# Two edits to a one-core kernel: when the next context is asked for, and how the first query is laid out

## What is computed

```python
h = jnp.concatenate([x, latents], axis=1)                 # 375 context rows, 112 latents
q = (latents @ q_w + q_b).reshape(b, k_len, NH, DH)       # 16 heads of 32
kv = (h @ kv_w + kv_b).reshape(b, p + k_len, NH, DH, 2)
attn = jnp.einsum('bkhd,bnhd->bhkn', q, kmat) / DH        # mask, softmax over n
attn_out = jnp.einsum('bhkn,bnhd->bkhd', attn, v).reshape(b, k_len, H)
attn_out = attn_out @ out_w + out_b + residual            # then RMS norm, MLP, + residual
```

## Time and profile before

| | us |
|---|---|
| median of three runs | 907.5 |
| lowest, highest | 907.29, 908.57 |
| the profiled execution | 907.18 |
| its span in the trace | 905.4 |
| PE busy | 857.8 (95%) |
| DVE, ACT, POOL busy | 567.1 (63%), 429.4 (47%), 228.5 (25%) |
| mean granted TensorE clock | 0.989 of full |

### The profile page before, as it was taken

The page is one execution under the profiler, slowest core; times in us unless marked ns, Lnnn a source line. Parts: engine busy times, 40 slices in busy tenths (PEclk is TensorE's granted clock), DMA queues, the critical chain, the costliest instruction groups (busy, mean ns, idle before and its releaser), DMA issues.

```text
span 905.4 us, 16349 instructions
## 1 busy us (share of the span) xinstructions
PE 857.8 (95%) x6220; PEld 671.0 (74%) x6220; DVE 567.1 (63%) x1318; ACT 429.4 (47%) x965; POOL 228.5 (25%) x242
## 2 busy tenths in 40 slices
PE   6777999999999988999999999999989999999998
PEld 5766777686867765676787777877767677888987
DVE  3499999999999989552233453333434365544654
ACT  3313242424242445344666685757656885333342
POOL 3546556464646458200000000000000000110100
PEclk9988999999999999999999999999999999999999
DMA  7657645554637253104002020202140231000200
GB/s 272 164 117 207 186 138 148 147 150 134 158 114 189 81 153 78 49 19 106 18 9 86 9 63 1 63 1 63 30 185 1 105 133 64 1 0 0 82 0 35
DMA packets 44421, 80.51 MB, mean 89 GB/s; under 512 B 21485, under 2 KB 27629, under 8 KB 42558
## 3 DMA queue, kind: packets, MB, share of 16 engines
q1 hardware_dynamic: 39742, 77.71, 29.8%
q10 hardware_dynamic: 4608, 1.84, 0.8%
HBM read 70.36 MB, written 9.18 MB: 88 GB/s over the span
## 4 chain that ended last, share of the span: by engine, by line
PE 46%; ACT 3%; DMA 1%; issue 1%; DVE 1%; SPq 0%; DVEq 0%
PE bank L1856 9%; PE bank L1843 8%; PE bank L1717 8%; PE bank L1723 7%; PE bank L1809 4%; PE bank L1801 3%; PE bank L1828 3%; PE bank L1765 2%; PE bank L1751 2%; ACT smb L1300 2%; DMA cx<-latc_scratch 1%; ACT pts L1308 1%; PE bank L1475 0%; PE bank L1817 0%; ACT cx_hi L1190 0%
## 5 line engine op out<-in xcount | busy, mean ns | idle before, releaser
L900 DVE CUSTOM_DVE_ANT_0 smb<-bank,mask 112x487 f32<-112x487 f32 x128 | 78.1, 660 | 126.1 <-issue 126.0
L693 DVE TENSOR_TENSOR_SCAN scan<-bank,scan 128x448 f32<-128x448 f32 x128 | 132.0, 1073 | 5.8 <-POOL scan L547 4.9
L1481 PEld LDWEIGHTS bank<-xj,front 128*128 128x128 f32 x1024 | 119.6, 196 | 10.1 <-issue 8.1
L544 POOL TENSOR_TENSOR scan<-scan,ks 128x896 f32<-128x896 f32 x64 | 124.2, 1940 | 2.3 <-DMA scan<-v_scratch 2.2
L1481 PE MATMUL bank<-xj,front 128*128 128x112 f32 x1024 | 121.9, 280 | 1.5 <-POOL xj L535 1.5
L1300 ACT ACTIVATE smb<-smb,nmax 112x487 f32<-112x487 f32 x128 | 88.3, 691 | 64.9 <-DVE nmax L900 64.5
L521 POOL TENSOR_TENSOR small<-small,neghalf 112x1 f32<-112x1 f32 x24 | 13.4, 559 | 362.4 <-DVE small L936 268.1
L700 DVE TENSOR_TENSOR scan<-scan,bank 128x896 f32<-128x896 f32 x64 | 68.8, 1078 | 1.8 <-PE bank L1481 1.0
L535 POOL TENSOR_TENSOR xj<-tmp,xa 128x448 f32<-128x448 f32 x40 | 42.4, 1062 | 86.1 <-DVE tmp L662 86.1
L1121 ACT ACTIVATE bank<-ws 128x448 f32<-128x448 f32 x32 | 17.5, 548 | 91.1 <-DVE scan L693 77.2
L1809 PE MATMUL bank<-ident,smb 112*122 112x112 f32 x512 | 56.6, 262 | 3.9 <-ACT smb L1300 3.5
(11 more groups left out here) (196 smaller groups left out, 1760.8 us busy)
## 6 DMA issues: line engine op xcount, KB each, us to landing
scan<-v_scratch SPq DMA_DIRECT2D x64, 448.0 KB, 5.5
cx<-in_ctxt SPq DMA_DIRECT2D x8, 750.0 KB, 5.2
raw_w<-in_wbig SPq DMA_DIRECT2D x4, 1024.0 KB, 7.8
w<-in_w SPq DMA_DIRECT2D x2, 2048.0 KB, 7.4
w<-in_w SPq DMA_DIRECT2D x1, 3328.0 KB, 11.7
tail<-in_wbig SPq DMA_DIRECT2D x3, 1024.0 KB, 9.2
front<-in_wbig SPq DMA_DIRECT2D x2, 1024.0 KB, 9.9
x_f<-in_x SPq DMA_DIRECT2D x8, 224.0 KB, 6.3
```

The costliest lines, as they stand in the source:

```text
L544: g.tensor_tensor(buf[:, :, :], buf[:, :, :], ks[b % 2][:, k:k + 1, 0:T].broadcast_to([P, VS, T]), ALU.mult).then_inc(s["a_ready"], 1)
L693: n = v.tensor_tensor_scan(flat, decay, flat, 0.0, ALU.mult, ALU.add)
L900: v.tensor_tensor_reduce(sm[r], bank[r][0:T, 0:NKEY], mask_b[b % 2][:, :], -1.0 / DH, 3e38, ALU.add, ALU.min, nmax[:, h:h + 1]).then_inc(s ...
L1481: i = t_.matmul(tiles(dst)[:, m, :], w[:, k, m * P:(m + 1) * P], x[:, k, :], start=k == 0, stop=k == NT - 1)
```

## The change

1. In SP's loop `load_context(b + 2)` moves from the end of the body to its top, ahead of `load_latents(b)`. Its own waits are the same.
2. `first_query` exchanges the operands. The stationary operand is now the latents (128 by 112), the moving one the 512 columns of a row of tiles of `qw`. The result is the query with tokens on partitions, in 12 products. ACT copies it to SBUF (`q_rows`, which lies where `lt` will be later), and PE turns it by four transposes (`first_query_turned`) into the same bank as before. On PE the transposes stand between `hidden_gate` and `hidden_values`. On ACT the copy stands where the bias was added; the bias now stands behind `second_gate`.
3. The pairs of semaphores `st`/`mv` of the layer norms become one each (`row_stats`), waited for at 2b + 1 and 2b + 2 in place of b + 1 of either. No instruction comes or goes by that.

```diff
@@ SP, the loop over the attentions
             for b in range(1, B - 1):
+                if real(b + 2):
+                    load_context(b + 2)
                 load_latents(b)
...
                 if real(b + 2):
-                    load_context(b + 2)
                     load_mask(b + 2)
@@ ACT
+            def first_query_rows():
+                act.wait_ge(s["q_rows"], 1)
+                c_.copy(q_rows[:, :], bank[7][0:T, :]).then_inc(s["q_rows_kept"], 1)
...
                 relu_squares(a_)
+                first_query_rows()
+                second_gate(a_)
                 first_query_columns()
-                second_gate(a_)
@@ PE
-                for m in range(NT):
-                    for k in range(NT):
-                        for w, c in in_parts(parts("qw"), x):
-                            i = t_.matmul(tiles(7)[:, m, :], w[:, k, m * P:(m + 1) * P], c[:, k, 0:T],
-                                          start=k == 0 and w is w_hi["qw"] and c is x[0],
-                                          stop=k == NT - 1 and w is w_lo["qw"])
-                i.then_inc(s["qp_ready"], 1)
+                for k in range(NT):
+                    for w, c in in_parts(parts("qw"), x):
+                        i = t_.matmul(bank[7][0:T, :], c[:, k, 0:T], w[:, k, :],
+                                      start=k == 0 and w is w_hi["qw"] and c is x[0],
+                                      stop=k == NT - 1 and w is w_lo["qw"])
+                i.then_inc(s["q_rows"], 1)
+
+            def first_query_turned():
+                pe.wait_ge(s["q_rows_kept"], 1)
+                turned(7, q_rows, "qp_ready")
...
                 first_query()
                 hidden_gate(a_)
+                first_query_turned()
                 hidden_values(a_)
```

More of the change, by code:

```diff
@@ L198, in build @@
         lt_lo = view("lt_lo", lt_at, [P, NT, T], F32R)
+        assert lt_at + C <= ROOM_S
+        q_rows = view("q_rows", lt_at, [T, C])
         kt[1] = room_s.take("kt1", [P, NT, NKEY])
@@ L255, in build @@
             ruk_ready rkp_ready y1_ready y_ready gmean gcen gsq gvar gsd grstd yn_ready
-            ya_ready yg_ready wo_ready x2_ready st2 mv2 ve2 rstd2 x2n_ready xcT_ready xc_ready sxc_ready xk_ready
+            ya_ready yg_ready wo_ready x2_ready row_stats2 ve2 rstd2 x2n_ready xcT_ready xc_ready sxc_ready xk_ready
             kkp_ready rrp_ready kk_relu kk_ready ffn_ready rrt_ready ffg lat_ready latT_ready latc_ready
-            lat_stored latc_stored st1 mv1 ve1 rstd1 init_pool init_dve wmix_loaded
+            lat_stored latc_stored row_stats1 ve1 rstd1 init_pool init_dve wmix_loaded
             wsplit_hi wsplit cx_loaded0 cx_loaded1 cx_hi_ready cx_ready kv_ready kv_kept qp_ready qt_ready
             mask_loaded0 mask_loaded1 mask_eq pad_ready s_done masked probs pt_ready pt_kept pvh rinv_heads rinv ri_ready ri_kept
-            ao_ready lt_hi_ready lt_ready lq_loaded lq_hi_ready lq_ready op_ready lat_back latob_ready x1_ready ve3 rstd3 x1n_ready h1T_ready h1_ready
+            q_rows q_rows_kept ao_ready lt_hi_ready lt_ready lq_loaded lq_hi_ready lq_ready op_ready lat_back latob_ready x1_ready ve3 rstd3 x1n_ready h1T_ready h1_ready
             w1_loaded w2_loaded b1_loaded b2_loaded lat_back0 lat_back1 lat_back2 lat_back3 latb2_ready hp_ready
@@ L627, in norm_start @@
             def norm_start(n, src, b):
-                v.bn_stats(stats[n - 1][:, :], src[:, :]).then_inc(s[f"st{n}"], 1)
-                dve.wait_ge(s[f"st{n}"], b + 1)
+                v.bn_stats(stats[n - 1][:, :], src[:, :]).then_inc(s[f"row_stats{n}"], 1)
+                dve.wait_ge(s[f"row_stats{n}"], 2 * b + 1)
                 v.memset(waiter[:, n - 1:n], 0.0)
-                v.bn_aggr(mv[n - 1][:, :], stats[n - 1][:, :]).then_inc(s[f"mv{n}"], 1)
-                dve.wait_ge(s[f"mv{n}"], b + 1)
+                v.bn_aggr(mv[n - 1][:, :], stats[n - 1][:, :]).then_inc(s[f"row_stats{n}"], 1)
+                dve.wait_ge(s[f"row_stats{n}"], 2 * b + 2)
                 v.tensor_scalar(small[n - 1][:, 0:1], mv[n - 1][:, 1:2], EPS_LN, None, ALU.add
```

## The result

| | kernel before | changed kernel |
|---|---|---|
| median | 908.11 us, 11 runs | 904.43 us, 11 runs |
| lowest to highest | 906.86 to 912.58 | 899.44 to 905.19 |
| profiled execution, its span | 907.18, 905.4 | 899.57, 897.8 |

The ratio is 0.9933, with a 95% interval of 0.9913 to 0.9954: faster by 0.7%, where 0.9% were forecast, and the median lies 3.1 us above the forecast range. The profiled execution, 899.57 us, lies within 0.5 us of the forecast. The median of eleven is the lowest time of the late group.

The account below looks back on a forecast made before the run. PE was taken to bound the kernel, with one stall in attention 5. 907.18 - 5.98 (context) - 2.22 (query) - 0 (semaphores) = 898.98, forecast as 899.1 us; own range 897.9 to 900.6, widened to 897.6 to 901.3.

Parts of the forecast that it names:

- What bounds the kernel, part 1: PE bounds; in attention 5, asking for the context at the loop's top removes PE's wait: -5.98 us.
- the event: Attention 5: context of sequence 7 lands late behind MLP weight, ACT's rounding and PE wait; price 5.98 us.
- What is late next in attention 5: nothing: Attention 5 without the wait becomes like attention 4, 40.10 us with PE busy 40.08.
- Part 2: Before the first scores, first query in rows: 5.39 - 2.77 - 0.40 = 2.22 us gained on PE.
- gap rule: First query's products by N/2.4 + 2.5 ns: part 2 would lose 0.6 us, total 901.8.
- ACT's schedule: Before attention 0: copy done at 409.1, bias at 413.7, queries wanted at 415.7; 2.0 us of slack.
- All later stages as long as before: After attention 0's first scores, at about 415.7, later stages keep their length; attention 5 is treated separately.
- How the numbers follow: Whole kernel: forecast chance 0.85; run scatter 0.3 below to 1.1 above the median; own range 897.9 to 900.6 us.
- A: Before first scores, query part pays nothing or loses 0.8 us: 901.2 or 902.0 us; chances 0.05 and 0.02.
- B: Attention 5's stall stays, the context being late for another reason: 905.0 us; chance 0.03.
- C: Slower: PE waits for ACT's copy in last_period, lower clock into attention 0; time near 933 if throughout; chance 0.02.
- D: In between or better: attention 0 shifts by tenths, part of the stall survives; 897.5 to 901 us; chance 0.03.

Follow-up runs that it names:

- e1: Kernel before with only load_context(b + 2) moved to the top of SP's loop; median 902.32 us, ratio 0.9934.
- e2: Changed kernel with the context's move undone, so only the first query is made in rows; median 906.02 us, ratio 0.9976.
- e5_before_spare: Kernel before plus 16 unread products in PE's idle stretch near 42 us; median 908.10 us, ratio 0.9993.
- e7: Changed kernel plus 16 unread products near 42 us and the first MLP weight's last 768 KB requested before the stored latents; median 901.13 us, ratio 0.9900.

## Why the prediction was right and wrong

- **What bounds the kernel, part 1: right.** The price of the event was taken whole, from two windows of equal work (46.08 - 40.10 = 5.98), with idle time and lower clock together; e1 measured 5.94. A reading of the waits alone would have given 3.5. "What is late next in attention 5: nothing" held too.
- **Part 2: right, to 0.02 us.** 2.22 forecast, 2.20 in eight traces. So close is in part luck: the 12 products took 2.84 us and not 2.77, and the transposes (0.38, not 0.40) and the gate (3.43, not 3.48) gave it back. The Trainium skill's gap rule (TensorE: Matmul & The Clock Gate, Back-to-back issue gap), which would have made this part a loss of 0.6, does not describe these products; the section itself gives that formula for an isolated product. The row of 5.39 us did describe them. ACT's schedule came out within 0.5 us of the one laid out.
- **"All later stages as long as before": wrong, 0.7 to 0.9 us.** This is the term missing in the sum: the stretch from the last attention's first scores to the end took 192.26 to 192.46 us and not 191.58. I counted what the new query does on the engines and did not ask what 36 fewer products and four more transposes (32 records fewer on PE, 6188 and not 6220) do to the times at which the program's own code is fetched. I had also not looked for margins near the end: the kernel before had its last weight piece 0.7 us ahead of need, which can be read from its rows (asked for at 740.95, landing 9.7 us later, 1.8 us of ACT's work behind it, PE there at 753.18).
- **"How the numbers follow", the scatter: wrong, and this put the median outside the range.** I took 0.3 below to 1.1 above the median from three runs, 907.29 to 908.57, and laid the range round one execution's time. Eleven runs of the same kernel then spread to 912.58, and 61 to 914.73. Stage one, which neither edit touches, takes 401 to 408 us; the two longest, 405.68 and 407.77, are in the two traces with the lowest mean clock, 0.980 and 0.981 where the other nine have 0.986 and more. So the failed term is the scatter: 1.1 us above the median were allowed, and in the kernel before 14 of 61 runs lie 4 to 7 us above. Whether the median lands in the range then hangs on how many of the runs at hand are late. Six of eleven were here; with the same kernel in two other sessions the medians were 901.23 and 900.26, inside the stated 897.6 to 901.3. The bounds also don't come out of their own terms, which give 898.2 to 900.9 round 898.98, where the prediction has 897.9 to 900.6. The page of before hinted at the scatter in its row of the clock, whose third and fourth slice are below 9:

```profile
PEclk9988999999999999999999999999999999999999
```

The prediction calls the stall in attention 5 "the one stall in the trace". That holds only behind stage one: near 42 us, in the same trace, PE idled 6.9 us, with the clock at 0.76 from 48 to 56 us. I had priced the lower clock only where the change was.

- **The rivals.** A (the query pays nothing) and B (the stall stays) are excluded by the table, C by the clock of 1.00 through attention 0 to 5. D had the right sign, some of the gain given back, but named another place. No rival spoke of a second group of times.

## What to carry to other kernels

Price a stall by the difference of two stretches with the same work, not by the wait: here idle time was 3.5 us and the price 6.0. Before giving a range, look where else in the program the clock drops in the profile at hand, since such stretches differ from run to run and may outweigh the edit; three runs do not show it, cutting several traces at the same marks does. And when a program gets shorter or longer, check the transfers with little margin near its end, since their company in the DMA queues changes.

## What the runs showed that I had not expected

- One block of code, 0.02 MB, falling inside a 2 MB transfer goes with a landing 0.7 to 1.4 us later (8.7 to 8.9 us in five traces against 7.5 to 8.0 in six); 32 fewer records on PE, more than 300 us earlier, had moved it there, and 32 put back moved it out again.
- The same unchanged instructions of stage one took 401.1 to 407.8 us. With the clock at 0.50 and 0.55 in the windows from 48 to 64 us it was 405.68 (e2); in e5_before_spare, at 1.00 and 1.00, it was 401.12. A second period with the lower clock, near 354 to 366 us, added 0.9 to 2.0 us in six traces of eleven.
- Filling an idle stretch of PE half (16 spare products) left the late runs in place; filling it whole left none in six runs, which may be chance, and its lowest time was 900.18 us, where e7's was 896.41.
